# Waiting for gathers by their own semaphores, and asking for ring places once in four groups: a graph attention kernel on one core

## What is computed

```python
xn = _layernorm(x, axis=-1)
# graph attention, 4 heads of 64:
xp = (x @ W).reshape(n, N_HEADS, HEAD_DIM)
e = leaky_relu(a_src[src] + a_dst[dst], 0.2)
e_exp = exp(e - segment_max(e, dst)[dst])
out = segment_sum((e_exp / segment_sum(e_exp, dst)[dst])[:, :, None] * xp[src], dst)
x = x + relu(out) + _L0_mix_ref(xn[None], ...)[0]      # linear attention over the nodes
x = x + _L0_ffn_ref(_layernorm(x, axis=-1)[None], ...)[0]   # 8 experts, each two layers and an output
```

## Time and profile before

| | |
|---|---|
| median of 3 runs | 4459.44 us (4455.92 to 4459.45) |
| profiled execution, span from first to last instruction | 3169.3 us |
| mean granted TensorE clock | 0.893 |
| PE busy | 2799.6 us (88%) |
| VectorE busy | 2292.7 us (72%) |
| ScalarE busy | 1531.0 us (48%) |
| GpSimd busy | 1491.4 us (47%) |

### The profile page before, as it was taken

The page is one execution under the profiler, slowest core; times in us unless marked ns, Lnnn a source line. Parts: engine busy times, 40 slices in busy tenths (PEclk is TensorE's granted clock), DMA queues, the critical chain, the costliest instruction groups (busy, mean ns, idle before and its releaser), DMA issues. The chain is left out here.

```text
span 3169.3 us, 61855 instructions
## 1 busy us (share of the span) xinstructions
PE 2799.6 (88%) x18584; PEld 2138.8 (67%) x18584; DVE 2292.7 (72%) x6615; ACT 1531.0 (48%) x4018; POOL 1491.4 (47%) x1580
## 2 busy tenths in 40 slices
PE   7777787888788998889888888879999999999999
PEld 6566676666667877777766777766666666666665
DVE  7587787878788787877888888885766665656633
ACT  3354465555555666656655655653333333333332
POOL 0777777777777777777777777720000000000000
PEclk9787787888778898889887887889999999999999
DMA  9544444444445555555544444433011010101000
GB/s 307 147 120 124 121 126 121 124 122 128 118 117 132 138 141 135 141 135 136 131 124 129 122 125 124 125 99 111 10 38 36 12 35 12 35 12 35 12 12 12
DMA packets 208686, 315.91 MB, mean 100 GB/s; under 512 B 84449, under 2 KB 142818, under 8 KB 208226
## 3 DMA queue, kind: packets, MB, share of 16 engines
q0 software_dynamic: 75360, 212.42, 25.9%
q1 hardware_dynamic: 125250, 92.39, 9.7%
q10 hardware_dynamic: 7744, 7.15, 0.7%
HBM read 279.46 MB, written 26.86 MB: 97 GB/s over the span
## 5 line engine op out<-in xcount | busy, mean ns | idle before, releaser
L755 POOL DMA_INDIRECT xg<-edge_table,idx x1564 | 1486.2, 950 | 523.0 <-issue 491.4
L1059 PE MATMUL ps_y<-y,hotw 128*128 128x260 f32 x3512 | 859.0, 407 | 69.9 <-issue 68.0
L1059 PEld LDWEIGHTS ps_y<-y,hotw 128*128 128x128 f32 x3512 | 689.9, 203 | 217.2 <-issue 81.6
L1809 DVE SCALAR_TENSOR_TENSOR xg<-ps_ye,wts,xg 128x256 f32<-128x256 f32 x392 | 189.7, 484 | 401.6 <-PE ps_ye L1599 401.4
L911 ACT ACTIVATE y<-xg,w 128x65 f32 x1756 | 463.3, 337 | 7.1
L1291 DVE TENSOR_TENSOR y<-xg,ps_v 128x780 f32<-128x780 f32 x439 | 417.0, 960 | 8.9 <-DVE ps_v L1284 0.5
L1642 ACT ACTIVATE tables<-ps_h,bnb,bns 128x448 f32<-128x448 f32 x224 | 162.3, 724 | 494.2 <-PE ps_h L1589 494.2
L970 ACT CAST hotw<-hot 128x512 f32<-128x512 bf16 x439 | 266.5, 622 | 246.4 <-PE ps_y L1059 246.0
L1599 PE MATMUL ps_ye<-wo,xg 128*128 128x256 f32 x1568 | 354.2, 383 | 0.2 <-DVE xg L1809 0.2
L1589 PE MATMUL ps_h<-xg,w 128*128 128x448 f32 x896 | 347.5, 541 | 1.0 <-issue 0.5
L1589 PE MATMUL ps_h<-tables,w 128*128 128x448 f32 x896 | 345.9, 539 | 0.0
(11 more groups left out here) (283 smaller groups left out, 3155.6 us busy)
## 6 DMA issues: line engine op xcount, KB each, us to landing
xg<-edge_table,idx POOLq DMA_INDIRECT x1564
mix_rows<-kk SPq DMA_DIRECT2D x49, 257.0 KB
xg<-mix_rows SPq DMA_DIRECT2D x7, 1799.0 KB, 8.4
xb<-in_xt SPq DMA_DIRECT2D x50, 128.0 KB
xnk<-in_x SPq DMA_DIRECT2D x50, 128.0 KB
x<-in_x SPq DMA_DIRECT2D x7, 896.0 KB, 11.4
xt<-in_xt SPq DMA_DIRECT2D x7, 896.0 KB, 13.4
xb<-in_xt SPq DMA_DIRECT2D x24, 256.0 KB
```

Source lines behind the costliest of these rows:

```text
L755: pool.indirect_dma_start(xg[:, q * OCT + u, j, :], None, dr["table"], bass.IndirectOffsetOnAxis(ap=idx[o % IDX][:, c:c + 1], axis=0)).the ...
L1059: mm = pe.matmul(ps_y[v % 2][:, 0:RW], hotw[v % 2][:, j, :], y[v % 2][:, j, :], start=(j == 0), stop=(j == CH - 1))
L1809: dve.scalar_tensor_tensor(yb[q][:, j, :], ps_y[j % 2][:, 0:D], wts[q][:, j, e:e + 1], yb[q][:, j, :], ALU.mult, ALU.add).then_inc(S["expe ...
```

## The change

`landed` is removed. GpSimd waits ahead of the first gather of a group until all gathers of its parity up to the group two before have landed. ScalarE and SP wait on both `got` semaphores themselves, so `need` becomes two lists, one for each parity, and `words` computes them in six operations in place of one. `PACE` becomes 4: `freed` is read once in four groups, and the wait is for four free places. The four list tiles have 124, 122, 125 and 77 rows in place of 128, 128, 128 and 64.

```diff
-VT = NVT // P + 1
+LIST = (124, 122, 125, 77)
+LAT = (0, 124, 246, 371)
+VT = len(LIST)
...
-RING, PACE = 16, 2
+RING, PACE = 16, 4
...
-        rows = [min(P, NVT - t * P) for t in range(VT)]
+        rows = LIST
...
-                            sp.dma_start(dr["dst"][t * P:t * P + rows[t], :], xrows[0:rows[t], t, 0:GE]).then_inc(stored, 16)
+                            sp.dma_start(dr["dst"][LAT[t]:LAT[t] + rows[t], :], xrows[0:rows[t], t, 0:GE]).then_inc(stored, 16)
...
-                    link(dve.tensor_scalar(K.need[:], grp[0:1, :], 1.0, float(ONE), ALU.add, ALU.add))
+                    for k in range(2):
+                        link(dve.tensor_scalar(slot_i[:], grp[0:1, :], 2.0 - k, None, ALU.add))
+                        link(dve.tensor_scalar(slot_i[:], slot_i[:], 1, None, ALU.arith_shift_right))
+                        link(dve.tensor_scalar(K.need[k][:], slot_i[:], 1.0, 16.0 * CH, ALU.max, ALU.mult))
...
+                        if not first or u >= 2:
+                            pool.wait_ge(got[u % 2], 16 * CH * ((o * OCT + u) // 2))
                         for j in range(CH):
-                            if j == CH - 1 and not (first and u == 0):
-                                pool.wait_ge(got[(u - 1) % 2], o * (16 * CH * OCT // 2) + 16 * CH * ((u - 1) // 2 + 1))
-                                pool.sem_inc(landed, 1)
...
-                    sp.wait_ge(landed, ONE + (o - IDX + 1) * OCT)
+                    for k in range(2):
+                        sp.wait_ge(got[k], 16 * CH * (o - IDX + 1) * OCT // 2)
...
-                        need.append(act.value_load(K.need[0:1, bass.ds(n(SV) + v, 1)], min_val=ONE + 1, max_val=ONE + NGP))
+                        need.append([act.value_load(K.need[k][0:1, bass.ds(n(SV) + v, 1)], min_val=16 * CH, max_val=16 * CH * NGP) for k in range(2)])
...
-                            act.wait_ge(landed, need[v > 0])
+                            for k in range(2):
+                                act.wait_ge(got[k], need[v > 0][k])
```

More of the change, by code:

```diff
@@ L288, in turn_groups @@
                     for t in range(VT):
-                        pe.transpose(ps_g[0:rows[t], t * P:(t + 1) * P], grp[:, t * P:t * P + rows[t]], ident).then_inc(gt_d, 1)
+                        pe.transpose(ps_g[0:rows[t], t * P:(t + 1) * P], grp[:, LAT[t]:LAT[t] + rows[t]], ident).then_inc(gt_d, 1)
                 def turn_lists(t):
@@ L386, in lists_out @@
                     act.wait_ge(last_t, t + 1)
-                    act.copy(K.last[:, t * GE:t * GE + r * CH].rearrange("p (v j) -> p j v", j=CH),
+                    act.copy(K.last[:, LAT[t] * CH:LAT[t] * CH + r * CH].rearrange("p (v j) -> p j v", j=CH),
                              ps_l[:, 0:GE].rearrange("p (j v) -> p j v", j=CH)[:, :, 0:r]).then_inc(lastc_d, 1)
@@ L510, in spreads @@
                     r = rows[t]
-                    at = slice(t * GE, t * GE + r * CH)
+                    at = slice(LAT[t] * CH, LAT[t] * CH + r * CH)
                     dve.wait_ge(rel_t, t + 1)
@@ L514, in spreads @@
                                       ps_r[:].rearrange("p (j v) -> p j v", j=CH)[:, :, 0:r],
-                                      bc(base[:, t * P:t * P + r], 1, CH), ALU.subtract).then_inc(rel_d, 1)
+                                      bc(base[:, LAT[t]:LAT[t] + r], 1, CH), ALU.subtract).then_inc(rel_d, 1)
                 def centre(i):
@@ L619 @@
     score_capped weights_done values_copied q_turned q_squared q_fourth mix_products mix_copied hot_widened y_done_act max_joined tail_first tail_second
-    tail_third pair_parts max_shifted max_leaky y_done y_summed acc_scaled acc_done asrc_packed iota_set weights_spread fold_spread groups_landed
+    tail_third pair_parts max_shifted max_leaky y_done y_summed acc_scaled acc_done asrc_packed iota_set weights_spread fold_spread
     k_products k_biased k_squared k_less k_scales k_normed k_sums_done k_sums_added k_columns_added one_set k_rooted kv_products kv_done root_bounded
@@ L684, in attend @@
          vo_d, qt_d, q2_d, q4_d, mix_d, mixc_d, hotw_d, ya_d, msum_d, tp1_d, tp2_d, tp3_d, pp_d, z1_d, lk1_d,
-         y_d, py_d, sc_d, acc_d, as_d, iota_d, wv_d, fov_d, landed,
+         y_d, py_d, sc_d, acc_d, as_d, iota_d, wv_d, fov_d,
          k_d, kb_d, k2_d, kr1_d, kr_d, kn_d, ka_d, kas_d, col_d, one_d, root_d, kv_d, kvs_d, lim_d, rec_d, kv1_d,
@@ L759, in _ @@
                     octet(o % 2, o, o == 0)
-                pool.wait_ge(got[(NG - 1) % 2], 16 * CH * ((NG + 1) // 2))
-                pool.sem_inc(landed, 1)
+                for k in range(2):
+                    pool.wait_ge(got[k], 16 * CH * ((NG + 1 - k) // 2))
                 for c in K.exp.values():
@@ L1848, in graph_layer @@
             K.blk, K.slot = ml.sb("blk", [1, NVT // 4], I32), ml.sb("slot", [1, NVT // 4], I32)
-            K.need = ml.sb("need", [1, NVT], I32)
+            K.need = [ml.sb(f"need{k}", [1, NVT], I32) for k in range(2)]
             K.freed = ml.sb("freed", [1, NGP // PACE], I32)
```

## The result

Slower, by 4.5%: 4661.26 us (median of 4 runs, 4653.75 to 4671.02) against 4459.44, ratio 1.0450 with a 95% interval of 1.0426 to 1.0474, so +201.8 us. I had forecast 4453.3. The profiled execution of the changed kernel took 4663.57 us with a span of 4661.8, so only 1.8 us lie outside the span. That alone refutes the way in which I carried 1290.1 us (and with it the sentence ahead of the prediction that they lie outside the instructions shown).

The account below looks back on a forecast made before the run. Attention was taken as gather-bound for its first 1500 us, almost balanced until 1960, then consumer-bound. Terms of -11.0, -0.1, +0.4, 0, 0, +0.6 and +4 sum to -6.1 us, giving 4453.3 us, range 4443 to 4470.

Parts of the forecast that it names:

- 1290.1 us: Difference between the profiled span, 3169.3 us, and the median time, 4459.44; claimed to lie outside the span and carried unchanged.
- The ring is never full when GpSimd asks: Attention's gather line: GpSimd's 23 waits naming a free ring place, 7.0 us in all, are only the normal gap.
- I take 0; bounds 0 and +5: Asking for free places once in four groups: loads saved on GpSimd are worth 0, a full ring is the possible cost.
- the lead of 5.6 us: Attention, tightest place found under the four-group ask: the needed multiplications end 5.6 us before the group's first gather.
- Landing waits: GpSimd's moved landing wait in attention: 11.4 us of stops gone, 11.0 us gained on the path, bounds 6 and 13.
- The list tiles: Preparation's gathers and stores: uneven sharing over DMA engines delays SP's x load; +4 us, lower end 0, upper +8.6.
- Rival (2): Preparation: the lists cost all 8.6 us and 3 more by holding up SP; sum +1.5, time 4461; chance 0.14.
- Words: Six operations for one on VectorE in the preparation: 2.1 us later, partly caught up; +0.6 us, bounds 0 and 2.1.
- ScalarE's own landing wait and loads: ScalarE in attention: seeing the landing itself -0.1 us, more waits +0.4, two more register loads a step 0.
- Rival (3): ScalarE's added register loads come out on attention's path: at 15 us the sum is +9.4, time 4468.8; chance 0.13.
- Pauses of 2.4 us: GpSimd's 13 pauses in the gather line, 112 gathers apart; forecast to stay, as no row ties them to a wait.
- Rival (4): The gather line's 13 pauses go too: 27 us more gained, time 4426; chance 0.05.

Follow-up runs that it names:

- e0: The kernel before, unedited, profiled again in a session where it is slow: 4516.52 us against 4514.37, span 4515.7.
- e8: The changed kernel, unedited, run again in a session where the kernel before takes 3170.15 us: 3175.93 us, ratio 1.0018.
- e12: The changed kernel with the old list tiles and PACE = 2, leaving only the waits changed: 4509.79 us against 4510.79, ratio 0.9996.
- e17: The changed kernel with the old list tiles and PACE = 1: no time, it needs more SBUF than there is.

## Why the prediction was wrong, point by point

- **"1290.1 us lie outside the span ... I carry them unchanged."** This is the step that failed. They were inside, in attention, in a regime that the trace shown did not have. The prediction named it as something that would make it wrong; it should have been read as a warning that trace and times were not of the same kind of execution, and the chances spread accordingly. What the runs showed in its place: e0 has a time of 4517.63 and a span of 4515.7, with 1350 us of GpSimd's waits for ring places in it.
- **"The ring is never full when GpSimd asks" and PACE "I take 0; bounds 0 and +5".** This is the term that came out wrong. True of the free regime: e8 has only gaps of 0.3 before the gathers that it puts down to a ring place. In the held regime GpSimd stops 96 times, nearly always for a ring place, and the term is +189. No rival covered it: I weighed a full ring only within the lead of 5.6 us.
- **Landing waits, -11.4 on GpSimd, 11.0 on the path.** On the gather line right in kind: no landing is named in e8. The size isn't shown: 13.3 us less than in the trace before, but that trace had the longest landing stops of the four free ones, and they differ by 11 us among themselves. On the path: nothing in the held regime (e12, 0.9996). In the free one it met a first gather 12.3 us late, and the last gather came 1.0 us earlier. Whether 11 would reach the end with the old tiles wasn't measured there.
- **The list tiles, +4, upper end 8.6 and 3 for SP's queue.** Measured: first gather +12.3 in e8, with x issued 9.1 us later; in the held regime 14 less -1, about 15 in time, give or take 12. Rival (2), at 11.6, had it, and its mechanism (rows and stores that hold SP's queue). The Trainium skill (DMA: Bandwidth & Descriptors, Why a DMA increments its semaphore by 16 and not by 1) gave fewer engines for such row counts; the later landing, 12.2 us in place of 6.5, agrees with it in direction, and the middle that I chose between it and even sharing was wrong. No run changes the row counts alone.
- **Words, +0.6, and ScalarE's own landing wait and loads, +0.3.** Hidden under the tiles in e8 and below the measurement in e12. Rival (3), loads on the path at 15 us or more, did not come. In e8 the time from multiplication to multiplication behind visits 3 and 4 keeps its median of 1.75 us, which is the sign that the prediction named, and e12 has no loss.
- **Pauses of 2.4 us**, as forecast, stay: the gather line of e8 has 13 again, 112 gathers apart. Rival (4) falls. (The prediction's "15 to 36 us" for them should be 21 to 36, by its own numbers.)

In its own regime the sum with rival (2)'s tiles is +1.5; measured +5.8 (0.09 to 0.28% of 3170, so 3 to 9). That the two are near is in part luck, as the gain of 11 isn't shown. In the regime of the times the sum missed the one term that made 94% of the result (189 of 202).

## What to carry to other kernels

Compare the span of a trace with the times before using either: in all other runs here they differ by about 2 us, and where they differed by 1290 the trace was of another regime. Terms costed at nothing "because nobody waits there" were the first to fail. Asking for several buffers at once was free only while the producer never stopped for one; where it did, bursts and stops became longer, +4.2% for 4 in place of 2. And a kernel that must run well in both regimes has a choice to make: a stop after every group costs 29% in the free one and gains 8% in the held one, while the finer ask (PACE = 1, on the kernel before) costs nothing in the one and gains 0.6% in the other. Together with the change's two lists of `need` (e17) it doesn't fit into SBUF.

## What was not expected of the hardware

- The same kernel takes 3163 us in one session and 4511 in another, within 1% inside each; without its gathers 3085 and 3145.
- In the held regime TensorE does 2.2 products a microsecond beside back-to-back gathers and 7.8 without them, and its increments arrive up to 15 us behind the recorded end of the product in the stretches I read; a stop of 2.6 us after every four gathers is enough for 4106 us in place of 4469.
- Row counts of 124, 122, 125 and 77 in place of 128, 128, 128 and 64 made the same 448 rows' gathers take 1438 ns (median) on GpSimd in place of 944, and land 12.2 us behind their issue in place of 6.5; SP's next load was issued 9.1 us later.
